# Rows of the attention stacks six partitions apart: a dimension's six products side by side

## The chip, the cores and the metric

The kernel runs on one core of a Trainium2 chip. The metric is the device time of one execution in microseconds. The core has TensorE (matrix products into PSUM), VectorE, ScalarE and GpSimd (called PE, DVE, ACT and POOL in the profile), SyncE (SP), which here issues nearly all DMAs, and 16 DMA engines that work off what is issued. SBUF has 128 partitions, that is rows.

## What is computed

The input x has 16 batches of 512 tokens with 256 features. Two layers are added to it: `x = x + layernorm(attention(layernorm(x)))` and then `x = x + layernorm(ffn(layernorm(x)))`, the second one a gated mixture of a dense branch and eight experts, two of them for each token. The change lies in the attention: 16 heads of 16 dimensions, over eight blocks of 64 tokens.

```
q = heads(h @ Wq.T + bq); k = heads(h @ Wk.T + bk); v = heads(h @ Wv.T + bv)
scores = einsum('bhqd,bhkd->bhqk', qx, kx) * scale
ctx    = einsum('bhqk,bhkd->bhqd', softmax(scores), vx)
```

The first and the last block of queries meet all keys, the others the first block, the last one and their neighbours.

## The kernel before

The program has three parts. `front` makes the attention and the routing of tokens in 16 + 3 steps, `experts` runs the experts over rows sorted by expert, and `last` mixes, normalizes and writes the result.

**A float32 product out of bf16 parts.** Q and K (each feature a row, each token a column) are cut into three bf16 parts (`split`, three parts side by side). A score is the sum of six products of parts, `Q_PART = [0, 0, 1, 1, 0, 2]` with `K_PART = [0, 1, 0, 1, 2, 0]`. To get all six in one matmul, they are laid along the contraction: a stack holds for each head 6 x 16 = 96 rows (`NGRP` groups of `DH` dimensions), then from `MASK_ROW` = 96 four mask rows and from row 124 rows of the row maximum. In the kernel before group g has rows 16g to 16g + 15. A matmul adds up over rows, so Q and K only have to use the same order.

**How the stacks are filled.** [...] For each batch, `put` (L531 to L532) writes the four blocks of split features to a buffer in memory, `split_spill` (m = 0: Q of heads 0 to 7, 1: K of these, 2 and 3: the same for heads 8 to 15), and `restack` (L534 to L541) fetches them back. One fetch takes one group g of one m: 16 dimensions by 8 heads by 512 columns in bf16, 128 KB, in pieces of 1 KB. There are six for each m, 24 for a batch and 384 in all. Each raises `s_stack[half]` when it lands. SyncE goes through one fixed list in each step: load x for the step after next, put 0, put 1, restack 0, put 2, restack 1, put 3, restack 2, restack 3, x again for the residual, rows of the dense branch, and at the end of the step eight DMAs with the row maxima.

**Who reads them.** The order of every engine is written out by hand in its own `step`. A step s projects batch s and takes its row maxima (`max_unit`, L723 on TensorE, followed by `maximum`, L1126, on VectorE), makes scores, exponentials and products for batch s - 1 (L743 on TensorE, L956 on ScalarE, L760 on TensorE), finishes batch s - 2 and routes batch s - 3. Routing has a part `dense` (L796, evicted by VectorE in L1156) in the PSUM banks `work` which the maxima use too. It begins in step 3. A step has 12 quads q; the units of the maxima begin in quad 3. The first one for a batch waits for `s_stack[0]`, all twelve fetches of m = 0 and 1, and for a free bank; the one of head 8 waits for `s_stack[1]`:

```python
if t == 0 and h % 8 == 0:
    pe.wait_ge(s_stack[h // 8], (b + 1) * 2 * NGRP * 16)
use(b, t, ("max", h))
```

In step 0 a matrix series (L655, L664) stands ahead of the units. The two stacks (even and odd batches) are in the space of the experts' weights w2 and w1, so the profile calls them `w`.

Of the kernel before, what the change touches and what calls it, by code (L numbers as in the profile page):

```python
# [26 lines left out]
HEADS, DH, BLK = 16, 16, 64  # L27
# [23 lines left out]
NGRP = len(Q_PART)  # L51
MASK_ROW = NGRP * DH
# [159 lines left out]
def front(nc, outer, a, z, kept, w1, w2, b1, b2):  # L212
# [7 lines left out]
    with ctx:  # L220
# [287 lines left out]
        def _(sp):  # L508
# [25 lines left out]
            def restack(b, par, m):  # L534
                half = m // 2
                st, parts = (kst, K_PART) if m % 2 else (qst, Q_PART)
                sp.wait_ge(s_spill[m], b * 16 + 16)
                for g, part in enumerate(parts):
                    src = spill[par, m].rearrange("(h d) s c -> d h s c", d=DH)[:, :, part, :]
                    sp.dma_start(st[par][g * DH:(g + 1) * DH, 8 * half:8 * half + 8, :], src)\  # L540
                      .then_inc(s_stack[half], 16)  # L541

            def store_abel(b, par):
# [16 lines left out]
            def step(s, par, i):  # L560
                if here(s, 0):
                    if not isinstance(s, int) or s + 2 < B:

                        sp.wait_ge(s_bn, (s + 1) * NTOK)
                        sp.wait_ge(s_xn, (s + 1) * NTOK)
                        plain(sp)
                        load_x(sp, xin[par], s + 2, s_xin[par])

                    wait(sp, s_sc, (s - 1) * UNITS)
                    plain(sp)  # L570
                    if isinstance(s, int) and s < 2:
                        sp.wait_ge(s_rows, 4)
                    put(s, par, 0)
                    put(s, par, 1)
                    restack(s, par, 0)
                    put(s, par, 2)
                    restack(s, par, 1)
                    put(s, par, 3)
                    restack(s, par, 2)
                    restack(s, par, 3)  # L580
# [1399 lines left out]
```

## Time and profile before

| | us |
|---|---|
| timed runs: median of 3 | 1988.91 |
| timed runs: lowest, highest | 1988.04, 1993.46 |
| profiled execution, its own time | 1984.16 |
| its span | 1982.3 |
| TensorE busy in the span | 1587.0 (80%) |
| VectorE busy | 1222.7 (62%) |
| ScalarE busy | 928.3 (47%) |
| GpSimd busy | 707.9 (36%) |

The profile comes from one execution, the profiled one, so sums of durations are held against its own time. The first 1206 us are nearly all attention steps of 67 to 77 us. In the views of waits and of the timeline, `[3.52 <-DMA w<-split_spill]` behind a row says how long the engine was idle before it and what ended this. PEclk is the granted TensorE clock: 1.00 is 2.4 GHz, 0.50 is 1.2 GHz. The DMA share is the mean busy share of the 16 DMA engines; packets overlap, so it can pass 1.

### The profile page before, as it was taken

The numbers are of one execution on the slowest core, as the hardware profiler recorded it, in microseconds if no ns is written. First come the engines' busy times: TensorE is split into PE (matmuls) and PEld (weight loads), VectorE is DVE, ScalarE is ACT, GpSimd is POOL, SyncE is SP. The second block draws the span as 40 slices with busy tenths as digits, with TensorE's granted clock in tenths as the row PEclk, the third lists the DMA queues.
The fourth block names the chain that finished last, engine by engine and source line by source line (L and its number), as shares of the span: only waits on it lengthen the run. The fifth ranks groups of instructions, "written<-read, shape, count | busy, mean of one in ns | idle before, by whom it ended". The sixth has DMA issues, their size and how long they took to land. (4 is left out here: it accounts for less than half of the span.)

```text
span 1982.3 us, 35750 instructions
## 1 busy us (share of the span) xinstructions
PE 1587.0 (80%) x10429; PEld 1070.9 (54%) x10430; DVE 1222.7 (62%) x3633; ACT 928.3 (47%) x1788; POOL 707.9 (36%) x716
## 2 busy tenths in 40 slices
PE   3878887887887887887888888849999999999700
PEld 2534444444444444444444444538888888888600
DVE  5746766766765765765766755334565556655367
ACT  1046556655755655655656646512333233323234
POOL 1011224313413413313324413522444444444558
PEclk9889999999999999999999998979999999999955
DMA  3453365275266275275265351574665566565387
GB/s 118 80 107 69 61 129 128 84 136 127 90 131 125 83 136 119 80 147 118 78 148 109 91 127 61 166 228 110 123 142 124 109 143 135 99 139 116 46 267 248
DMA packets 185577, 241.78 MB, mean 122 GB/s; under 512 B 24585, under 2 KB 156049, under 8 KB 185297
## 3 DMA queue, kind: packets, MB, share of 16 engines
q1 hardware_dynamic: 158544, 203.58, 41.3%
q0 software_dynamic: 26880, 36.33, 11.0%
q8 instruction: 76, 1.25, 0.3%
q14 instruction: 77, 0.62, 0.1%
HBM read 133.40 MB, written 105.91 MB: 121 GB/s over the span
## 5 line engine op out<-in xcount | busy, mean ns | idle before, releaser
L956 ACT ACTIVATE pexp<-scT 128x512 f32<-128x512 f32 x768 | 440.7, 599 | 361.6 <-PE scT L743 351.8
L1126 DVE TENSOR_REDUCE mx<-work 128x1 f32<-128x320 f32 (+2 forms) x1024 | 493.1, 548 | 59.8 <-PE work L723 57.5
L1603 POOL DMA_INDIRECT y_rows<-rows_add,row_of x144 | 228.6, 1588 | 296.2 <-DMA y_rows<-rows_add,row_of 221.6
L743 PE MATMUL scT<-w 128*128 128x192 bf16 (+3 forms) x1536 | 274.4, 277 | 55.0 <-ACT pexp L956 54.3
L723 PE MATMUL work<-w 126*128 126x320 bf16 (+4 forms) x1280 | 268.0, 302 | 61.9 <-DVE mx L1126 26.6
L1635 PE MATMUL h_ps<-inT,w1c 128*128 128x256 f32 x1152 | 262.2, 381 | 2.4 <-DVE inT L1687 2.4
L1648 PE MATMUL o_ps<-w,hT 128*128 x1152 | 260.4, 379 | 0.0
L1635 PEld LDWEIGHTS h_ps<-inT,w1c 128*128 128x128 f32 x1152 | 219.8, 191 | 33.1 <-issue 2.9
L743 PEld LDWEIGHTS scT<-w 128*128 128x128 bf16 x1536 | 125.0, 98 | 204.4 <-ACT pexp L956 144.2
L1578 ACT ACTIVATE rows_add<-rows_out,row_share 128x257 f32<-128x257 f32 x144 | 65.5, 503 | 355.1 <-DVE rows_out L1703 270.8
L1648 PEld LDWEIGHTS o_ps<-w,hT 128*128 128x128 f32 x1152 | 213.4, 190 | 26.1
L1399 POOL DMA_INDIRECT z_rows<-z,to_row x128 | 125.4, 980 | 227.1 <-DVE to_row L1221 107.9
L723 PEld LDWEIGHTS work<-w 126*128 126x128 bf16 x1280 | 110.3, 98 | 164.3 <-DVE mx L1126 78.0
L1378 POOL TENSOR_TENSOR split<-resid,split 128x512 bf16<-128x512 f32 x64 | 73.4, 1158 | 241.6 <-ACT split L928 241.6
L1696 DVE TENSOR_TENSOR rows_out<-o_ps,b 128x512 f32<-128x512 f32 x72 | 49.9, 692 | 159.5 <-PE o_ps L1648 159.5
L1386 POOL TENSOR_TENSOR x<-x,ctxn 128x256 f32<-128x256 f32 x64 | 46.5, 728 | 242.1 <-ACT ctxn L947 242.1
L700 PE MATMUL work<-xnT,wqkv 128*128 128x512 f32 x256 | 124.0, 631 | 9.6 <-issue 8.9
L1570 ACT ACTIVATE hT<-h_ps,b1c 128x256 f32<-128x256 f32 x288 | 112.4, 464 | 37.6 <-PE h_ps L1635 37.6
L1110 DVE SCALAR_TENSOR_TENSOR resid<-work,bqk_sb,split 128x512 f32<-128x512 f32 x64 | 47.6, 750 | 100.8 <-ACT split L923 81.4
L1137 DVE RECIPROCAL rden<-turn 128x16 f32<-128x16 f32 x64 | 15.7, 246 | 150.9 <-PE turn L775 150.9
L760 PE MATMUL pv<-pexp,vaug 128*32 128x192 f32 (+3 forms) x1536 | 104.6, 391 | 1.2 <-ACT pexp L956 0.9
L760 PE MATMUL pv<-pexp,b 128*32 128x192 f32 (+3 forms) x1536 | 104.5, 391 | 0.0
(173 smaller groups left out, 2164.4 us busy)
## 6 DMA issues: line engine op xcount, KB each, us to landing
w<-split_spill SPq DMA_DIRECT2D x384, 128.0 KB, 6.1
split_spill<-split SPq DMA_DIRECT2D x64, 384.0 KB, 4.1
rows_in<-z_rows SPq DMA_DIRECT2D x72, 265.0 KB, 4.7
y_rows<-pre SPq DMA_DIRECT2D x16, 514.0 KB, 6.9
y<-y_rows SPq DMA_DIRECT2D x16, 514.0 KB, 6.7
x_rows<-x SPq DMA_DIRECT2D x16, 512.0 KB, 2.8
abel_rows<-pre SPq DMA_DIRECT2D x16, 512.0 KB, 5.8
abel_in<-abel_rows SPq DMA_DIRECT2D x16, 512.0 KB, 4.5
```

The lines of the kernel that those rows point to most:

```text
L700: ins = nc.tensor.matmul(work[w][:, :], wqkv[:, k, col:col + P], xnT[:, k, :], start=(k == 0), stop=(k == KC - 1))
L723: ins = nc.tensor.matmul(work[t][:, at:at + hi - lo], tile(qst[par][0:K_SCORE, h, :], t), kst[par][0:K_SCORE, h, lo:hi], start=True, stop= ...
L743: ins = nc.tensor.matmul(scT[n % 2][:, at:at + hi - lo], tile(kst[par][0:K_EXP, h, :], t), qst[par][0:K_EXP, h, lo:hi], start=True, stop=True)
L760: ins = nc.tensor.matmul(pv[32 * n:32 * n + 32, lo:hi], vaug[par][:, t, h, :], pexp[:, (q * GROUP + n) % NPB, at:at + hi - lo], start=(c = ...
L956: nc.scalar.activation(pexp[:, (q * GROUP + n) % NPB, :], scT[n % 2][:, :], ACT.Exp, scale=DH ** -0.5).then_inc(s_exp, 1)
L1126: nc.vector.reduce_max(mx[:, c:c + 1], work[t][:, 0:n], AX_X).then_inc(w_free[t], 1)
L1378: nc.gpsimd.tensor_tensor(split[:, m, 2, :], resid[:, m % 2, :], split[:, m, 1, :], ALU.subtract).then_inc(s_split, 1)
L1399: pool.indirect_dma_start(kept.z_rows, bass.IndirectOffsetOnAxis(ap=idx, axis=0), zb[bp][:, j, :], None).then_inc(g_scat[bp], 16)
L1570: nc.scalar.activation(hT[par][:, f, :], h_ps[par][:, f * RT:(f + 1) * RT], ACT.Gelu, bias=b1c[par][:, f:f + 1]).then_inc(e_hT, 1)
L1603: pool.indirect_dma_start(kept.y_rows, bass.IndirectOffsetOnAxis(ap=row_of[n][:, r:r + 1], axis=0), rows_add[n % 2][:, r, :], None, comput ...
L1635: ins = nc.tensor.matmul(h_ps[par][:, f * RT:(f + 1) * RT], w1c[par][:, k, f * P:(f + 1) * P], inT[par][:, k, :], start=(k == 0), stop=(k ...
L1648: ins = nc.tensor.matmul(o_ps[par][:, r * D:(r + 1) * D], hT[par][:, f, r * P:(r + 1) * P], w2[:, bass.ds(e, 1), f, :].rearrange("p o d -> ...
```

## The change

The destination of a fetch steps over partitions. Group g had rows 16g to 16g + 15 and now has rows g, g + 6, ..., g + 90; dimension d of a head, with its six products, lies in rows 6d to 6d + 5. The source, the size of a fetch, the number of fetches, their order and all other instructions are as before. Line numbers after it are one higher.

```diff
                 for g, part in enumerate(parts):
                     src = spill[par, m].rearrange("(h d) s c -> d h s c", d=DH)[:, :, part, :]
-                    sp.dma_start(st[par][g * DH:(g + 1) * DH, 8 * half:8 * half + 8, :], src)\
+
+                    sp.dma_start(st[par][g:MASK_ROW:NGRP, 8 * half:8 * half + 8, :], src)\
                       .then_inc(s_stack[half], 16)
```

## Rows read from the trace of the kernel before

**Rows 1.** Busy time by stretch, a middle step: start:end, length, engines, clock, DMA.
```profile
core 0: us, PE busy (x) PEld busy (x) DVE busy (x) ACT busy (x) POOL busy (x), PEclk, DMA share, GB/s
...
608.00:683.00 75.00, 59.17 (x478) 32.90 (x474) 49.19 (x142) 45.06 (x80) 24.55 (x27) 0.98 0.50 115
```
**Rows 2.** Line L723: min/median/max ns, first and last start in us, shapes.
```profile
L723 PE MATMUL work<-w x1280: 217/301/635, 74.4 to 1202.4; 126*128 126x320 bf16 x37, 126*128 126x384 bf16 x37, 126*128 126x192 bf16 x37, 126*128 126x512 bf16 x36
```
**Rows 3.** Line L540, the fetches, whole span: waits (us, times) and landing.
```profile
  PEld work L723: 9.7, 3
  PE work L723: 7.3, 2
...
DMA to landing us min/median/max: 2.9/6.1/9.9
```
**Rows 4.** Timeline of SyncE, step 1: start us, us, instruction.
```profile
117.12 2.68 SPq L540 DMA_DIRECT2D w<-split_spill  x6
```
**Rows 5.** Line L540, twelfth fetch alone, of steps 1, 2 and 9: issue, landing.
```profile
L540 SPq DMA_DIRECT2D w<-split_spill x1: 431/431/431, 122.8 to 122.8; - x1
...
DMA to landing us min/median/max: 7.7/7.7/7.7
...
L540 SPq DMA_DIRECT2D w<-split_spill x1: 431/431/431, 192.1 to 192.1; - x1
...
DMA to landing us min/median/max: 7.6/7.6/7.6
...
L540 SPq DMA_DIRECT2D w<-split_spill x1: 425/425/425, 700.7 to 700.7; - x1
...
DMA to landing us min/median/max: 8.1/8.1/8.1
```
**Rows 6.** Timeline of TensorE, steps 1 and 2: start us, us, instruction, [idle before].
```profile
130.49 1.20 PE L723 MATMUL work<-w 126*128 126x320 bf16 x3 [3.52 <-DMA w<-split_spill]
...
135.27 0.53 PE L723 MATMUL work<-w 126*128 126x384 bf16 x1
...
199.69 1.19 PE L723 MATMUL work<-w 126*128 126x320 bf16 x3 [3.77 <-DMA w<-split_spill]
...
204.47 0.47 PE L723 MATMUL work<-w 126*128 126x384 bf16 x1
```
**Rows 7.** Timeline of TensorE, the same units in step 3, and step 9.
```profile
266.47 0.80 PE L723 MATMUL work<-w 126*128 126x320 bf16 x3 [1.36 <-DVE pre L1156]
...
269.15 0.33 PE L723 MATMUL work<-w 126*128 126x384 bf16 x1
...
709.58 0.89 PE L723 MATMUL work<-w 126*128 126x320 bf16 x3 [1.43 <-DVE pre L1156]
```
**Rows 8.** Timeline of VectorE, step 2 and step 9.
```profile
197.80 0.15 DVE L1063 SCALAR_TENSOR_TENSOR x_shift<-mv,rstd 128x4 f32<-128x4 f32 x1
...
203.60 1.95 DVE L1126 TENSOR_REDUCE mx<-work 128x1 f32<-128x320 f32 x4 [1.84 <-PE work L723]
...
709.08 0.78 DVE L1156 TENSOR_TENSOR pre<-work,bias_ab 128x265 f32<-128x265 f32 x2
```
**Rows 9.** Clock, DMA share and GB/s by stretch (columns as in rows 1).
```profile
129.70:136.40 6.70, 5.91 (x37) 2.55 (x38) 3.58 (x7) 1.48 (x3) 0.00 (x0) 0.50 1.15 190
197.90:204.70 6.80, 5.01 (x34) 2.27 (x35) 2.74 (x7) 0.60 (x1) 0.00 (x0) 0.50 1.13 212
266.40:272.40 6.00, 4.62 (x41) 2.81 (x42) 4.18 (x9) 1.67 (x3) 0.00 (x0) 1.00 1.16 193
246.50:249.50 3.00, 3.00 (x11) 1.42 (x10) 2.42 (x6) 1.51 (x4) 1.73 (x2) 1.00 0.30 89
553.10:561.00 7.90, 6.09 (x62) 3.93 (x66) 7.09 (x24) 3.66 (x7) 2.53 (x4) 1.00 1.14 211
1892.00:1900.00 8.00, 0.00 (x0) 0.00 (x0) 2.64 (x9) 1.88 (x3) 0.00 (x0) 0.50 1.00 370
...
704.00:712.00 8.00, 6.54 (x68) 4.04 (x61) 6.86 (x23) 2.99 (x6) 2.53 (x4) 1.00 1.15 175
```

## The prediction

> **What bounds the kernel now.** I read the page first, then a table by stretch, then the waits around the fetches, and last the timeline of single steps. The attention part ends with its last unit of the row maxima, at 1202.4 us; experts and last pass, the 780 us behind it, use neither stacks nor fetches, and the change costs or gives them nothing [rows 2]. In a middle step of the attention TensorE is busy for 59 of 75 us and VectorE and ScalarE for less, so TensorE's own order of work, with its small waits, sets the pace [rows 1].
>
> The question is whether anybody waits for a fetch. Each step issues 24 of them: six for Q of heads 0 to 7, six for their K, twelve for the other heads. TensorE's units for the maxima (L723) begin when the first twelve have landed. In the whole span TensorE waits for a fetch twice, 7.3 us; the weight loads' three waits, 9.7 us, are mostly the same time seen on their side [rows 3].
>
> The two are in steps 1 and 2. In step 1 the last of the twelve is issued at 122.8 and takes 7.7 us, to 130.5; TensorE idles 3.52 us until 130.49. In step 2 it is 192.1 + 7.6 = 199.7, and TensorE idles 3.77 us until 199.69 [rows 5, 6]. Together 7.29 us: these are all of [rows 3]. From step 3 on `dense` of an older batch stands ahead of the units. In step 9 the last of the twelve lands at 700.7 + 8.1 = 708.8, but the unit starts at 709.58, just behind the first of the two evictions at 709.08 (0.78 us for both) that frees its bank [rows 5, 7, 8]. In step 0 a matrix series stands ahead and no wait on TensorE is put down to a fetch. So 14 of 16 steps have nothing to gain from an earlier landing.
>
> **The change part by part.** The instructions are the same in kind, count and order on every engine: 384 fetches of 16 rows by 8 heads by 512 columns. Only the destination rows differ: 16 rows six apart in place of 16 adjacent ones. Q and K are permuted alike and the mask rows keep their places, so each matmul has the same shape; those, the row loads of the maxima and SyncE's order cost nothing more or less.
>
> *Duration of a fetch.* While nearly only fetches are in flight, 553.1 to 561 us, the transfer engines are always busy (share 1.14, over 1 since packets overlap) and move 211 GB/s: 211/(16 x 1.14) = 11.6 GB/s for each engine, and 128 KB take 131072/(16 x 11.6) = 0.71 us. Rows of x, 1 KB too, but spread over 64 or 128 partitions, go at 89/(16 x 0.30) = 18.5 GB/s: 0.44 us for the same bytes [rows 9]. The size of a row is equal; what differs is how many destination rows a transfer has and how full the queue is. My choice is the faster rate, since 16 engines that write into 16 adjacent rows is the only odd thing about the fetches, and their rows now lie over 91 partitions. The bounds are 0.71 us (rows not to blame) and, from the last pass with 4 KB rows, 370/(16 x 1.00) = 23 GB/s, 0.35 us. SyncE issues six fetches in 2.68 us, 0.45 us each [rows 4], so anything under that gives no more. Twelve fetches then save 12 x 0.27 = 3.2 us until the last lands; none to 3.8 us are the ends.
>
> The Trainium skill, SBUF — State Buffer, Door 1: The DMA port swizzle, says that bandwidth goes by how many of 16 ports the partitions reach; 16 adjacent ones reach four (measured there at 104 GB/s). By its map 16 rows six apart reach 13 ports with at most two rows each, so a fetch should fall from 1.26 us to about 0.6 us, an estimate from that page; twelve would save over 7 us and both waits would go whole, 11.8 us in the sum. The trace agrees in direction only: packed fetches take 0.71 us, not 1.26.
>
> *Steps 1 and 2, the waits.* 3.52 us shrink to about 0.3 us and 3.77 us to about 0.6 us. All of this lies on the path: VectorE has no unit to take a maximum of and ScalarE gets no scores, since these stand behind the units on TensorE.
>
> *Steps 1 and 2, the clock.* During each wait the granted clock fell to 0.50, that is 1.2 GHz in place of 2.4, and stayed there: 129.7 to 136.4 and 197.9 to 204.7 [rows 9]. TensorE had been idle for 2.7 us (since 126.97) and 2.0 us (since 195.93) by then. In step 3, after 1.36 us without work, it stayed at 1.00 [rows 6, 7, 9]. The same instructions (three units, 24 of L760, a score, four units, a score, a unit) took 135.80 - 130.49 = 5.31 us in step 1 and 204.94 - 199.69 = 5.25 us in step 2, against 269.48 - 266.47 = 3.01 us in step 3 [rows 6, 7]. With the wait shortened to half a microsecond I expect no fall: 2.3 us and 2.2 us. The ends are nothing and these.
>
> *What is late next.* In step 1 nothing: VectorE and ScalarE are free. In step 2 VectorE finishes other work only at 197.95, so its maxima start then. The last four of the first seven end at 205.55 and take 0.49 us each; seven such are 3.4 us and would end at about 201.6 with a short wait between [rows 8]. That is 3.9 us for step 2 instead of 3.2 + 2.2 = 5.4.
>
> **Sum.** Step 1: 3.2 + 2.3 = 5.5 us. Step 2: 3.9 us. Together 9.4 us. The profiled execution took 1984.2 us (span 1982.3) and would take 1974.8; the median of the timed runs, 1988.9, is 0.24% above it and becomes 1979.5. The other DMAs of a step (x for the residual, the abel rows, the second twelve fetches) go out earlier or at the same time; none of them is waited for on TensorE before [rows 3], so earlier costs and gives nothing.
>
> **The rivals.**
> *The rows are not what slows a fetch* (0.15). The spilled source is read in pieces of 1 KB out of 3 KB. If reading sets 0.71 us, nothing moves: 1988.9 us. For it: packets queue at share 1.14 and a lone row of x does not. Against it: a fetch lands 2.9 us after issue at best, 6.1 in the median and up to 9.9 [rows 3], so it is the piling up that makes it late, at a rate which x shows can be higher. The Trainium skill, DMA: Bandwidth & Descriptors, Where 436 GB/s comes from, has the memory side bind in such loads, at about 358 GB/s; the fetches move 211, so by this trace that limit is not reached.
> *A half gain* (0.17). The fetch falls to 0.6 us, waits shrink by 12 x 0.11 = 1.3 us each, and the idle time still ends in a lower clock: 2.6 us, about 5 if one fall goes: 1984 to 1986.3 us.
> *Slower* (0.08). Nothing in this trace shows a transfer into rows six apart. If such rows make a fetch slower, I take it to reach the worst rate seen among them, 175/(16 x 1.15) = 9.5 GB/s from 704 to 712 us [rows 9], 0.86 us, 1.9 us later for twelve. Steps 1 and 2 pay 1.9 each. Step 9 has 709.6 - 708.8 = 0.8 us to spare and pays 1.1; if all 13 steps behind step 2 were as tight, 14.3 us. I take a quarter of these, 3.6: 7.4 us in all, 1996.3. It decides as soon as the last of twelve takes over 7.7 us to land.
> *More than forecast* (0.08). Both waits go whole, no cover by VectorE, 3.5 + 3.8 + 2.3 + 2.2 = 11.8 us: 1977.1, and some of the short falls of the clock elsewhere go too.
>
> **How the numbers follow.** The forecast has 0.52. About 0.3% (6.0 us) is what a measurement of this kernel can tell from no change. Faster by more: 0.52 + 0.08, and 0.02 from the half gain: 0.62. Within: 0.15 + 0.15 + 0.01 = 0.31. Slower: 0.07. The range goes from 1975.5 (all of it, and 1.6 us of spread between runs) to 1988.9, the time of no effect; both sides beyond hold under 0.2.
>
> **What would show it.** The median landing of the fetches falls from 6.1 us to about 4 [rows 3]; the last of twelve in step 1 lands under 5 us after issue; the rate per engine in the fetch stretch rises towards 18 GB/s; L723 waits for a fetch under 2 us in all; the clock stays 1.00 around 130 and 200 us; the middle steps keep 75 us. I am wrong if landing stays at 6 us, if the clock falls anyway, or if other steps change by over 1 us.

## The result and the profile after

The changed kernel took 1982.97 us in the median of 20 runs (1976.90 to 1989.28), the kernel before 1993.12 us in 20 runs beside it (1984.20 to 1998.76). The ratio is 0.9954 with a 95% interval of 0.9942 to 0.9966: faster by 0.46%, 9.2 us, between 6.8 and 11.6 (the two medians differ by 10.2 us). The profiled execution took 1985.26 us, its span is 1983.4. In a second comparison on another occasion the ratio was 0.9946 (0.9926 to 0.9966).

The profile shown before the prediction took 1984.16 us, less than any of the 20 timed runs of its kernel. So the two spans say nothing about the change (1982.3 against 1983.4), and both kernels had to be profiled again to tell why.

The fetches (line L541 now) over the whole span, as [rows 3] has them; the three numbers behind x384 are SyncE's time to issue one, in ns, min/median/max:

```profile
L541 SPq DMA_DIRECT2D w<-split_spill x384: 554/600/1928, 48.1 to 1159.9; - x192
...
  PEld work L724: 3.9, 3
  PE work L724: 1.5, 2
...
DMA to landing us min/median/max: 2.5/2.9/4.7
```

The median landing was 6.1 us [rows 3] and is 2.9. The waits of TensorE for a fetch are down from 7.3 to 1.5 us. But SyncE now needs 0.60 us to issue a fetch. Its timeline in step 1, which answers to [rows 4]:

```profile
116.72 3.87 SPq L541 DMA_DIRECT2D w<-split_spill  x6
120.63 0.59 SPq L532 DMA_DIRECT2D split_spill<-split  x1
121.26 3.79 SPq L541 DMA_DIRECT2D w<-split_spill  x6
```

Six fetches take 3.87 us of SyncE's time, 0.65 us each with the gap between two, where they took 2.68. The put behind them also costs more, 0.59 us in place of 0.43. TensorE in steps 1 and 2, which answers to [rows 6]:

```profile
127.58 0.69 PE L724 MATMUL work<-w 126*128 126x320 bf16 x3 [1.27 <-DMA w<-split_spill]
...
130.15 0.33 PE L724 MATMUL work<-w 126*128 126x384 bf16 x1
...
192.53 0.99 PE L724 MATMUL work<-w 126*128 126x320 bf16 x3 [0.23 <-DMA w<-split_spill]
...
195.39 0.39 PE L724 MATMUL work<-w 126*128 126x512 bf16 x1 [0.26 <-DVE mx L1127]
...
195.85 0.34 PE L724 MATMUL work<-w 126*128 126x384 bf16 x1
```

The waits are 1.27 and 0.23 us where they were 3.52 and 3.77. The run of units, products and scores behind them takes 130.48 - 127.58 = 2.90 us (5.31 before) and 196.19 - 192.53 = 3.66 us (5.25 before). In step 2 a wait for VectorE shows up, 0.26 us. The granted clock and the DMA engines by stretch (start:end, length, five engines, clock, DMA share, GB/s), which answers to [rows 9]:

```profile
129.60:136.30 6.70, 5.66 (x38) 3.05 (x36) 5.29 (x11) 3.86 (x7) 0.00 (x0) 1.00 0.59 176
191.00:197.80 6.80, 5.21 (x50) 2.29 (x53) 6.26 (x20) 4.24 (x9) 2.53 (x4) 1.00 0.81 246
...
553.10:561.00 7.90, 6.38 (x64) 4.01 (x58) 6.75 (x22) 2.88 (x6) 2.54 (x4) 1.00 0.72 213
```

The clock stays at 1.00 behind both waits. In the stretch from 553.1 to 561 us the same traffic (213 GB/s against 211) keeps the engines busy for a share of 0.72 where it was 1.14: 213/(16 x 0.72) = 18.5 GB/s for each engine, where it was 11.6. This is the rate while an engine's packets are in flight, by the share; it is not what all 16 deliver over the stretch, which is the same in both.

Where did the time come from? The eight small DMAs with the row maxima mark the end of every step. From those of step 0 to those of step 2 (steps 1 and 2), and from there to those of step 15 (the 13 steps behind):

```profile
106.17:241.46 135.29, 111.96 (x866) 59.99 (x868) 83.57 (x191) 75.90 (x140) 22.52 (x24) 0.94 0.44 87
241.46:1205.44 963.98, 787.13 (x6134) 441.45 (x6126) 647.94 (x1845) 571.34 (x1010) 315.90 (x334) 0.99 0.51 113
```

for the kernel before, and for the changed one

```profile
105.71:232.85 127.14, 107.32 (x858) 58.67 (x868) 83.14 (x191) 75.92 (x140) 22.47 (x24) 0.98 0.29 93
232.85:1208.80 975.95, 793.10 (x6090) 446.45 (x6134) 648.83 (x1845) 571.67 (x1010) 316.57 (x334) 0.98 0.35 112
```

Steps 1 and 2 are 8.2 us shorter. The 13 steps behind them are 12 us longer in this pair of profiles, and the experiments have to say whether the change does that.

### The profile page after: what moved, and what is told of

Read it like the earlier page. It is cut to its first block and busy times, and to the rows that moved or that the text cites. A ratio compares the mean times of both kernels' runs of the same rounds, so it can differ in the third digit from the quotient of the medians.

```text
span 1983.4 us, 35686 instructions
## 1 busy us (share of the span) xinstructions
PE 1583.6 (80%) x10365; PEld 1071.7 (54%) x10430; DVE 1223.3 (62%) x3633; ACT 928.6 (47%) x1788; POOL 709.1 (36%) x716
## 5 line engine op out<-in xcount | busy, mean ns | idle before, releaser
L744 PE MATMUL scT<-w 128*128 128x192 bf16 (+3 forms) x1472 | 257.0, 272 | 63.3 <-ACT pexp L957 57.5
L1400 POOL DMA_INDIRECT z_rows<-z,to_row x128 | 125.8, 983 | 228.5 <-DVE to_row L1222 108.4
L701 PE MATMUL work<-xnT,wqkv 128*128 128x512 f32 x256 | 130.3, 658 | 9.7 <-issue 9.0
```

The lines of the kernel that those rows point to most:

```text
L701: ins = nc.tensor.matmul(work[w][:, :], wqkv[:, k, col:col + P], xnT[:, k, :], start=(k == 0), stop=(k == KC - 1))
L744: ins = nc.tensor.matmul(scT[n % 2][:, at:at + hi - lo], tile(kst[par][0:K_EXP, h, :], t), qst[par][0:K_EXP, h, lo:hi], start=True, stop=True)
L1400: pool.indirect_dma_start(kept.z_rows, bass.IndirectOffsetOnAxis(ap=idx, axis=0), zb[bp][:, j, :], None).then_inc(g_scat[bp], 16)
```

## The experiments

My theory: the change is worth what it takes off the waits of steps 1 and 2 and off the lower clock behind them. The main rival: quicker transfers help a little in every step, or cost something there. Each kernel ran beside the kernel before on the same chip, and its ratio is to that. An edit can shift line numbers by one to three, so the units of the maxima are L723 to L726 and the fetches L540 to L542.

### Only batches 1 and 2, and all but these

```diff
             def restack(b, par, m):
+                apart = isinstance(b, int) and b in (1, 2)
...
-                    sp.dma_start(st[par][g * DH:(g + 1) * DH, 8 * half:8 * half + 8, :], src)\
+                    at = slice(g, MASK_ROW, NGRP) if apart else slice(g * DH, (g + 1) * DH)
+                    sp.dma_start(st[par][at, 8 * half:8 * half + 8, :], src)\
```

The second kernel has `not (...)` around the condition.

> Only batches 1 and 2 get rows six apart; the other 14 keep adjacent rows. My theory (the change is worth what it takes off the waits of steps 1 and 2, with the clock behind them): the whole gain, ratio 0.994 to 0.997, some 6 to 11 us; in the profile the two waits of L723 shrink from 3.5 and 3.8 us to about 1.2 and 0.5, and the row loads of step 3 begin near 307 us instead of 315. Rival (faster fetches help a little in every step): two of sixteen steps, so a gain of about 1 us, ratio 0.999 to 1.000.

> The complement: batches 1 and 2 keep adjacent rows, the other 14 get rows six apart. My theory: no gain, ratio 0.999 to 1.001, with the waits of 3.5 and 3.8 us still there. Rival (a little in every step): 14/16 of the gain, ratio 0.995 to 0.997. A third reading (SyncE's slower issue, 0.60 instead of 0.43 us for each fetch, costs something in the middle steps, which the whole change nets off): slower than before by 1 to 4 us, ratio 1.0005 to 1.002.

Measured: 0.9948 (0.9923 to 0.9974) for the two batches alone, medians 1984.1 against 1994.4 us; 1.0001 (0.9981 to 1.0021) for the other fourteen. Steps 1 and 2 in their profiles, two batches alone ahead, the other fourteen below:

```profile
105.48:232.67 127.19, 107.01 (x858) 58.69 (x868) 83.17 (x191) 75.89 (x140) 22.39 (x24) 0.98 0.30 92
```
```profile
106.34:242.24 135.90, 111.20 (x858) 60.28 (x868) 83.53 (x191) 75.88 (x140) 22.51 (x24) 0.94 0.45 86
```

TensorE waits 1.40 and 0.89 us in the one, 3.73 and 3.21 us in the other. The gain sits in two batches of sixteen, as far as the intervals tell, and the rival falls. So does its other form: fourteen batches with fetches that take SyncE 0.60 us and land after 3.0 us neither gain nor cost anything that can be measured, within 0.2%.

### Other steps between the rows

```diff
-                    sp.dma_start(st[par][g * DH:(g + 1) * DH, 8 * half:8 * half + 8, :], src)\
+                    at = slice(g, 64, 4) if g < 4 else slice(60 + g, MASK_ROW, 2)
+                    sp.dma_start(st[par][at, 8 * half:8 * half + 8, :], src)\
```

> Groups 0 to 3 have rows four apart (in rows 0 to 63), groups 4 and 5 rows two apart (in 64 to 95). By the Trainium skill's map (SBUF page, Door 1) 8 ports for each fetch, two rows each. Theory A (what makes an adjacent fetch slow is that its 16 rows meet in too few ports): fetches are as quick as with six apart, landing 2.9 to 3.5 us. Theory B (a step of six was special): landing stays at 6 us. On SyncE's issue: if it is slow for any step over rows it is 0.60 us here too; if it is slow because six is no power of two, it is 0.43 us, the twelfth fetch of steps 1 and 2 lands about 1 us sooner than with six apart, no wait is left, and the ratio is 0.993 to 0.996.

Measured: 0.9969 (0.9947 to 0.9992), medians 1985.9 against 1994.4 us. TensorE waits 0.95 and 2.12 us, and steps 1 and 2 take 126.8 us, as in the changed kernel (127.1). The clock stayed at 1.00 behind both waits. The fetches in its profile:

```profile
L541 SPq DMA_DIRECT2D w<-split_spill x384: 537/600/2176, 48.9 to 1162.0; - x192
...
DMA to landing us min/median/max: 2.6/3.5/5.3
```

The first part went as theory A has it: six was not special; rows four and two apart land nearly as quickly, 3.5 us. By the Trainium skill's map (SBUF — State Buffer, Door 1: The DMA port swizzle) such a fetch reaches 8 ports with two rows each, one six apart 13 or 14 with at most two. The trace agrees with more ports being quicker (3.5 and 2.9 us). No run separates ports from the mere distance between the rows. On the issue, the idea that six is slow because it is no power of two falls: four and two cost 0.60 us as well, so the hope of no wait left fell with it. In all three spacings the issue costs 0.17 us more than with adjacent partitions. Why the put behind such fetches is issued more slowly too (0.59 us) stays open, since its own rows are as before.

### The put behind the fetches of K

```diff
-                    put(s, par, 2)
                     restack(s, par, 1)
+                    put(s, par, 2)
                     put(s, par, 3)
```

> Adjacent rows as before; SyncE issues the six fetches of K (m = 1) before put 2 rather than behind it, so 384 KB fewer lie ahead of the twelfth fetch. Put 2 keeps the 16 DMA engines busy for about 2 us. My theory (only the landing of the twelfth fetch in steps 1 and 2 is worth anything, by whatever means): it lands some 2 us sooner, the waits shrink to 1 to 2 us each, and the gain is 4 to 9 us, ratio 0.9955 to 0.998. Rival (what helps is the shorter total DMA time, 32% in place of 41% of the engines): nothing, ratio 0.999 to 1.001, since the DMA work is the same.

Measured: 1.0005 (0.9983 to 1.0026), and waits of 3.52 and 4.16 us. My sub-theory on the put was wrong: the twelfth fetch lands no sooner. SyncE in step 1 of this kernel:

```profile
117.55 5.52 SPq L540 DMA_DIRECT2D w<-split_spill  x12
```

The first fetch lands 3.1 us after its issue, at 120.7. The last is issued at 122.6 and takes 8.2 us, the longest of the twelve. So they land from 120.7 to 130.8: eleven intervals in 10.1 us, 0.92 us for each fetch. From first issue to last landing it is 13.3 us. In the kernel before, with a put between, it is 13.3 us too. The stretch of the landings, in this kernel and then in the kernel before:

```profile
120.70:130.80 10.10, 5.21 (x47) 2.63 (x46) 0.76 (x2) 4.44 (x8) 0.00 (x0) 0.96 1.15 166
```
```profile
120.20:130.40 10.20, 5.74 (x48) 2.63 (x46) 0.76 (x2) 4.55 (x9) 0.00 (x0) 0.96 1.13 208
```

In the same time, at the same share, the engines of the kernel before move 208 GB/s in place of 166. They carry the put along, and the twelve land no later for it. Why, no run shows; that the put reads SBUF and a fetch writes it is only a guess at the reason. It also means that the price of a fetch depends on what is counted. Over the whole trace two fetches in a row land 0.83 us apart in the median in the kernel before, with puts among them, and 0.97 us in this kernel. My price, 0.71 us, came from the rate in a stretch in which a put was moved as well (issued at 551.50, landed at 558.2), whose bytes the GB/s count.

### Another order of the groups

```diff
-                for g, part in enumerate(parts):
+                for g in (0, 1, 4, 5, 2, 3):
+                    part = parts[g]
```

> Adjacent rows as before and SyncE's quick issue, but the six groups of a block are fetched in the order 0, 1, 4, 5, 2, 3. By the Trainium skill's map (SBUF page, Door 1) groups 0 and 2 share four ports and so do 1 and 3, while 4 and 5 have others. Theory A (fetches in flight together delay each other where they share ports): four groups in a row on different ports, landing falls from 6.1 us to 4 to 5.5, the two waits to 1.5 to 3 us, ratio 0.996 to 0.999. Theory B (a fetch into 16 adjacent rows is slow by itself, whatever comes before it): landing 6 us, waits as before, ratio 0.999 to 1.001.

Measured: 0.9997 (0.9980 to 1.0015); waits 3.52 and 3.56 us. The fetches:

```profile
L541 SPq DMA_DIRECT2D w<-split_spill x384: 302/431/1582, 49.3 to 1165.4; - x192
...
DMA to landing us min/median/max: 2.9/5.9/9.7
```

Theory B holds for this order: the landing stays, though neighbours in the queue write other rows. What crowds is then most likely the 16 rows of one fetch among themselves. That is argued from two orders and three spacings; how they crowd no run here shows.

### The landing held back with quick fetches

```diff
                     put(s, par, 2)
+                    if isinstance(s, int) and s in (1, 2):
+                        sp.wait_ge(s_spill[2], s * 16 + 16)
                     restack(s, par, 1)
```

on the changed kernel.

> Rows six apart everywhere, but in steps 1 and 2 SyncE waits for the landing of put 2 (some 3.3 us after its issue) before it fetches K of heads 0 to 7. So the transfers are as quick as in the changed kernel, and only the twelfth landing of these two steps is late again, by about 2.7 us. My theory (that landing, and the clock that falls behind a long wait, is all the change is worth): waits of L724 of about 4.0 and 2.9 us, the granted clock at 0.50 again behind at least one of them, and most of the gain gone, ratio 0.997 to 1.000. Rival (the gain comes from quicker transfers as such): ratio 0.994 to 0.996 as for the change.

Measured: 1.0000 (0.9982 to 1.0018), medians 1989.36 against 1989.11 us. The units of steps 1 and 2 and the two steps as a whole:

```profile
132.13 1.19 PE L726 MATMUL work<-w 126*128 126x320 bf16 x3 [3.85 <-DMA w<-split_spill]
...
202.08 0.69 PE L726 MATMUL work<-w 126*128 126x320 bf16 x3 [3.02 <-DMA w<-split_spill]
```
```profile
107.32:243.22 135.90, 112.88 (x866) 60.54 (x868) 83.60 (x191) 75.89 (x140) 22.43 (x24) 0.94 0.27 86
```

The fetches land as quickly as in the changed kernel (2.9 us in the median, 4.3 at most), and yet the gain is gone: 135.9 us, as before. The lower clock is back with the waits (0.94): in step 1 it fell during the wait, in step 2 at 202.8 us, 0.7 us behind its end. This is the complement of the kernel with two batches only. Together they pin the gain down to the landing of the twelfth fetch in steps 1 and 2. The hold also delays all that SyncE issues behind it in these steps; but the two waits shown are the only ones of TensorE for a fetch in this profile too.

### The load of x behind the fetches, without and with the change

```diff
                 if here(s, 0):
-                    if not isinstance(s, int) or s + 2 < B:
-                        sp.wait_ge(s_bn, (s + 1) * NTOK)
-                        sp.wait_ge(s_xn, (s + 1) * NTOK)
-                        plain(sp)
-                        load_x(sp, xin[par], s + 2, s_xin[par])
...
                     restack(s, par, 1)
+                    if not isinstance(s, int) or s + 2 < B:
+                        sp.wait_ge(s_bn, (s + 1) * NTOK)
+                        sp.wait_ge(s_xn, (s + 1) * NTOK)
+                        plain(sp)
+                        load_x(sp, xin[par], s + 2, s_xin[par])
```

> Adjacent rows as before; SyncE loads x for the step after next behind the fetches of K (m = 1) instead of ahead of put 0. Put 0 is ready at 113.4 and 181.2 us in the trace of before and issued at 114.5 and 183.8, so the twelfth landing comes 1.1 us sooner in step 1 and 2.5 in step 2. My theory: waits 2.4 and 1.3 us, the lower clock gone behind the second, 3.6 us without and 5.8 us with a fall saved: ratio 0.997 to 0.9985. Rival (only the layout counts): 0.9995 to 1.001.

> Both: rows six apart and the load of x behind. What is left of the waits in the changed kernel is 1.27 and 0.23 us; both should go. My theory: 1 to 1.5 us better than the change, ratio 0.9935 to 0.9955 to before. Rival (x comes too late for its own use, the statistics of VectorE): slower than the change by some us, with waits of VectorE's L1054 for x in the profile.

> Rows six apart and the load of x behind the fetches, once more and beside the changed kernel. Steps 1 and 2 took 124.3 us in its profile against 127.2, so I expect a median 1 to 3 us below after_again's; equal medians would say that the 3 us are given back later.

Alone it gave 0.9983 (0.9964 to 1.0001): unclear, with the waits unchanged at 3.54 and 4.10 us and steps 1 and 2 at 136.0 us, so not for my reason. The twelfth fetch was issued at 120.7 in place of 122.8, but took 9.0 us, and the twelve took 14.7 us from first issue to last landing where they had taken 13.3. Counted from the row loads of step 0, the last landed 0.2 us sooner. The load of x now stands right behind the fetches and lands at 129.8 to 131.0, so its packets are in flight together with theirs; whether this is what slows them no run isolates. With rows six apart it does what I said: no wait in step 1, 0.64 us in step 2, steps 1 and 2 down to 124.3 us, and 124.7 us in its second profile. In time that is 0.9957 (0.9936 to 0.9977) and, beside the changed kernel on the same chip, 0.9944 (0.9924 to 0.9963) against its 0.9946: medians 1982.0 and 1982.0 us. Beside 127.1 and 125.8 us for the changed kernel the 1 to 3 us are there in the profiles, and the timing cannot show them. I would not call it better. The rival did not happen: VectorE waits for the load of x 2.2 us over the whole span, and 2.4 in the changed kernel.

### The same kernels profiled again

> The kernel before, unchanged, for a second profile. Its first profile took 1984.2 us, its timed runs 1993 in the median; in it the 13 steps behind step 2 took 964.0 us with 30.7 us at the lower clock in all of the attention from 110 to 1200 us, the changed kernel's profile 976.0 us with 44.4. My theory (these falls come by chance of the execution, the first profile was a lucky one): steps 1 and 2 again near 135 us and two waits of 3.5 to 3.8 us, but 968 to 977 us behind them. Rival (the change makes the later steps longer by 12 us): 964 us again.

> The kernel before once more: as before_again. Two profiles with 962 to 966 us for the 13 later steps would speak for a cost of the change there, values spread over 964 to 977 us for chance.

> The changed kernel, unchanged: a second profile and a comparison on one chip with the version below. Ratio to before 0.994 to 0.997. Steps 1 and 2 together 127 us; the 13 steps behind them 966 to 978 us if chance sets them, 976 again if the change does.

The 13 steps behind step 2, in the second and third profile of the kernel before (whole executions 2006.85 and 1995.79 us):

```profile
242.74:1229.10 986.36, 804.37 (x6094) 451.59 (x6139) 648.59 (x1845) 571.82 (x1010) 316.00 (x335) 0.97 0.50 111
```
```profile
241.19:1218.59 977.40, 795.28 (x6090) 447.37 (x6134) 648.48 (x1845) 571.61 (x1010) 315.86 (x334) 0.98 0.49 112
```

and in the second of the changed kernel:

```profile
106.88:232.65 125.77, 105.64 (x858) 58.20 (x868) 83.25 (x191) 75.92 (x140) 22.39 (x24) 0.99 0.30 94
232.65:1210.70 978.05, 795.78 (x6090) 447.54 (x6134) 648.49 (x1845) 571.67 (x1010) 315.89 (x334) 0.98 0.34 112
```

964.0, 986.4 and 977.4 us before, 976.0 and 978.0 us after. VectorE, ScalarE and GpSimd are busy for the same time to 1 us in all five; what differs is the clock, 0.99, 0.97 and 0.98. The traces say for how long it was at the lower level in these 13 steps. Over all 14 profiles of this text the 13 steps take 957.7 us and 0.43 us for each microsecond at the lower clock, and none is more than 1.3 us off this line. So profiles with the same time at the lower clock can be set side by side, with rows adjacent or six apart in these steps:

| at the lower clock, us | rows adjacent, us | rows six apart, us |
|---|---|---|
| 17.6, 17.1 | 964.0 (before) | 964.7 (the other fourteen) |
| 34.1, 34.1 | 972.2 (two batches alone) | 972.8 (x later, second profile) |
| 47.9, 47.8 | 977.4 (before, third) | 978.1 (changed, second) |

The changed kernel's first profile had 41.0 us at the lower clock and the one of before 17.6: 23.4 us x 0.43 = 10 of the 12 us, and the rest is no more than the line's own scatter. The pairs differ by 0.6 to 0.7 us, and that is all that the change can be seen to do to these 13 steps.

The early steps scatter less: 135.3, 136.3 and 134.9 us before, 127.1 and 125.8 us after. The difference of the means, 135.52 - 126.46 = 9.1 us, stands beside 9.2 us by the timed runs. The single waits scatter more than their sum: TensorE waits 3.52 and 3.77, 3.69 and 4.10, 2.88 and 5.07 us before, which is 7.3 to 8.0 us in all; 1.27 and 0.23, 0.77 and 1.41 us after, 1.5 and 2.2 us in all.

## Why the prediction was right

**The place.** Right. Steps 1 and 2 hold all of the gain, the other fourteen none: shown from both sides by the two kernels with part of the batches.

**Step 1, 5.5 us forecast.** Measured 68.6 - 63.8 = 4.8 us in the first pair of profiles (from the row loads of step 0, at 106.17 and 105.71, to those of step 1, at 174.79 and 169.48). Within it the wait fell by 2.25 us, not 3.2, and the run behind it by 2.4 us, forecast 2.3.

**Step 2, 3.9 us forecast.** Measured 66.7 - 63.4 = 3.3 us. The wait fell by 3.5 us (3.2 forecast) and the run behind it by 1.6 us (2.2 less the cover by VectorE). That is more than 3.3: in this execution the clock was at the lower level from 169.8 to 173.2 us, at the start of step 2, and TensorE came to its wait 22.8 us behind the row loads of step 1 where it had been 21.1. In the second profile, without such a fall there, step 1 is 63.7 and step 2 is 62.1 us.

**The sum.** 9.4 us forecast; 9.2 us by the ratio, with 6.8 to 11.6 as its interval; 9.1 us by the means of three and two profiles. The time itself, 1979.5, was 3.5 us too low, since the kernel before measures 1993.1 us in 20 runs and not the 1988.9 of three. Three runs that spread over 5 us were too few to set a level by.

**The duration of a fetch.** Two errors that went against each other, and that the sum came out is in part luck. Before the change the twelve land 0.93 us apart, a put among them (120.2 to 130.4 us), and 0.92 with the put behind, not 0.71. After it the DMA engines do reach 18.5 GB/s each by their share, the very rate taken from the rows of x, 0.44 us for 128 KB. But the fetches come 0.65 us apart, because SyncE needs 0.60 us to issue one where I had written that SyncE's order would "cost nothing more or less" and that anything under 0.45 us gives no more. That SyncE's issue is the floor was right; its size was wrong, because I carried over the issue time of adjacent rows. From 0.92 to 0.65 us is 0.27 us for a fetch, which is by accident what I had from 0.71 to 0.44, and 12 x 0.27 = 3.2 us was forecast. Measured from the first issue to the twelfth landing in step 1: 13.3 us before, 10.8 after, 2.5 us less. Part of the difference is the put between the fetches: before, the fetches landed no later for it, now its 0.63 us of SyncE's time, gap included, stand in the row.

**The estimate by ports.** My estimate from the Trainium skill (SBUF — State Buffer, Door 1: The DMA port swizzle) had a fetch at 1.26 us before and 0.6 after, and both waits gone. The trace does not agree on the size: before it takes 0.92 us in the kernel with the put behind, 142 GB/s, over the 104 that the Trainium skill gives, and waits of 1.5 us are left. It agrees on the direction: more rows apart, quicker; two, four and six all quick. The map has the first four groups on 13 ports and the last two on 14, with at most two rows for each, so the estimate does not change by this. The estimate for after, 0.6 us, cannot be held against the trace, since SyncE's issue hides what a fetch by itself would take.

**The clock.** Right: with waits of 1.27 and 0.23 us it stayed up, and also with 0.77 and 1.41 us in the second profile and 0.95 and 2.12 us in the kernel with other spacings. With 3.52 and 3.77 us it fell, and with quick fetches and waits of 3.85 and 3.02 us it fell again. The two runs behind the waits became 4.0 us shorter by it, beside 5.8 us for the waits themselves. The two make 9.8 us, and the later arrival in step 2 takes 1.7 of them back: 8.1 us, for 8.2 measured in this pair.

**What was said of the rivals.** *The rows are not what slows a fetch* is out: the engines' rate rose. *Slower* is out: the largest landing fell from 9.9 to 4.7 us. *A half gain* rested on 0.6 us for a fetch, and that price came close (0.65), but the fetch before was dearer than it assumed and the clock did not fall. *More than forecast* needed both waits gone, and 1.5 us of them are left. The sign "other steps change by over 1 us" did not come either, once profiles with the same clock are compared.

## What to carry to other kernels

Look for who waits on a transfer before pricing it: here 384 transfers land in half the time, and only the two landings that somebody waited for were worth anything. A wait of 3 to 4 us on TensorE costs more than itself, since the lower clock behind it cost 1.4 to 2.4 us more in the six cases of the three profiles of before: runs of 4.3 to 5.3 us, where the changed kernel has 2.9. Where a load writes few rows of SBUF (16 here), lay them apart rather than side by side, and expect its issue to cost more. When profiles of one execution differ by more than the change, profile both kernels again before explaining the difference, and compare stretches that spent the same time at the lower clock.

## What the runs showed of the hardware

- SyncE issues a DMA of 16 rows by 8 x 512 bf16 in 0.43 us when the rows are adjacent and in 0.60 us when they are six apart, or in the other kernel four and two apart (medians of 384 in each kernel).
- Fetches of 128 KB into 16 adjacent rows, queued one behind the other, land 0.92 us apart in step 1 of the kernel with the put behind (0.97 us in the median of its whole trace). Twelve of them take 13.3 us there from first issue to last landing, and 13.3 us with a put of 384 KB between; another order of groups leaves the median landing at 5.9 us. With rows six apart an engine goes from 11.6 to 18.5 GB/s by its share on the same traffic.
- Issuing sooner into this queue was worth nothing: with x loaded later, the twelfth fetch went out 2.1 us sooner and took 9.0 us in place of 7.7. Twelve fetches then took 14.7 us and not 13.3.
- TensorE waited 2.12 us in one kernel and 1.41 us in another and kept the clock of 1.00; waits of 2.88 us and more all had a fall to 0.50 during them or within 0.7 us behind.
- The time of one and the same kernel, the one before, went from 1984.2 to 2006.9 us in three profiled executions, with a granted clock over the span of 0.947 in the first and 0.937 in the slowest. In 14 profiles of kernels with equal work, 13 steps of the attention took 964 to 986 us, 0.43 us more for each microsecond at the lower clock (17 to 68 us), within 1.3 us. Why one execution spends more time at the lower clock than another stays open.
